# Paged attention on one core: copies of the cache spread differently over SyncE's and ScalarE's queues, and the first layer's weights of a row fetched whole

## The reference: what is computed

```python
# layer 0: each row picks one of 16 weights
x = x + einsum('bsi,boi->bso', x, weight[adapter_ids])          # 512 x 512 per row
# layer 1: attention with a paged cache
q, k, v = x @ Wq.T, x @ Wk.T, x @ Wv.T       # 32 query heads, 8 key heads, D = 128
q, k = rope(rmsnorm(q)), rope(rmsnorm(k))
kc, vc = k_cache[block_table], v_cache[block_table]   # 16 pages of 32 keys per row
scores = q @ concat(kc, k).T * SCALE         # 512 cached + 128 new keys, masked
x = x + (softmax(scores) @ concat(vc, v)) @ Wo.T
```

## Time and profile before

| | |
|---|---|
| median of 3 runs | 1103.47 us (1098.93 to 1104.15) |
| profiled execution | 1106.2 us |
| its span in the trace | 1104.4 us |
| TensorE busy | 1033.2 us, 94% of the span |
| VectorE, ScalarE, GpSimd busy | 79%, 73%, 69% |
| mean granted clock of TensorE | 0.978 |
| copies into `cache_rows` | 96 issued by SyncE, 32 by ScalarE |

### The profile page before, as it was taken

How to read it: one execution, slowest core, us unless ns; L and a number is a source line. 1 busy time by engine, 2 the same in 40 slices (tenths; PEclk the granted TensorE clock), 3 DMA queues, 4 the chain that set the end, 5 groups by cost and what they waited for, 6 DMA issues and landing times.

```text
span 1104.4 us, 19826 instructions
## 1 busy us (share of the span) xinstructions
PE 1033.2 (94%) x5500; PEld 877.1 (79%) x5500; DVE 868.8 (79%) x1999; ACT 803.2 (73%) x2094; POOL 758.8 (69%) x794
## 2 busy tenths in 40 slices
PE   7799897999999999999998999999998999899996
PEld 5587776888877888788887888788887888788874
DVE  6565555566887988898887998888898898888893
ACT  3364445555787887888787887888888887888883
POOL 1876656466476777877776776777777776777753
PEclk8999999899999999999999999999999999999999
DMA  6687767988667788788878887678877788777884
GB/s 202 185 251 233 213 185 202 242 246 212 132 139 151 141 162 149 137 152 147 159 138 148 145 162 151 144 145 147 161 144 151 143 159 148 138 147 141 149 154 98
DMA packets 477839, 180.87 MB, mean 164 GB/s; under 512 B 420753, under 2 KB 457762, under 8 KB 475682
## 3 DMA queue, kind: packets, MB, share of 16 engines
q1 hardware_dynamic: 474464, 167.61, 73.8%
q10 hardware_dynamic: 2242, 9.89, 2.9%
q0 software_dynamic: 1024, 2.10, 0.6%
HBM read 109.25 MB, written 35.66 MB: 131 GB/s over the span
## 4 chain that ended last, share of the span: by engine, by line
PE 52%; SPq 16%; DVE 11%; DMA 8%; issue 6%; POOL 4%; ACT 3%; POOLq 0%; DVEq 0%; ACTq 0%
PE S L1221 12%; PE O L1155 5%; SPq L394 5%; DVE pr L939 4%; SPq L349 4%; PE O L1156 4%; PE O L1157 4%; DMA first<-pr 4%; PE Q L1155 3%; PE Q L1157 3%; PE Q L1156 3%; POOL ptl L515 3%; SPq L404 3%; PE Y L1155 3%; PE Y L1157 3%
## 5 line engine op out<-in xcount | busy, mean ns | idle before, releaser
L921 DVE CUSTOM_DVE_ANT_0 pr<-S,mask,rst 128x640 f32<-128x640 f32 x256 | 225.5, 881 | 65.1 <-PE S L1221 58.9
L737 ACT ACTIVATE pr<-pr,nb 128x640 f32<-128x640 f32 x256 | 211.5, 826 | 32.0 <-DVE nb L921 31.6
L939 DVE SCALAR_TENSOR_TENSOR pr<-pr,rc,raw 128x640 f16<-128x640 f32 x208 | 229.7, 1105 | 5.0 <-ACT raw L722 4.9
L722 ACT ACTIVATE raw<-pr,rc 128x640 f16<-128x640 f32 x208 | 170.9, 822 | 0.1
L540 POOL TENSOR_TENSOR m<-m 128x512 f32<-128x512 f32 x64 | 111.4, 1740 | 70.4 <-DVE m L967 69.1
L1155 PE MATMUL O<-pth,vh 128*128 128x512 f32 x256 | 111.5, 436 | 40.5 <-POOL ptl L515 33.8
L494 POOL TENSOR_TENSOR kl<-raw,kh 128x512 fp32r<-128x512 f32 x64 | 97.6, 1526 | 66.5 <-ACT kh L622 65.2
L515 POOL TENSOR_SCALAR ptl<-first 128x512 fp32r<-128x512 f16 x130 | 94.0, 723 | 55.1 <-DMA first<-pr 46.6
L682 ACT ACTIVATE Q<-Q 128x128 f32<-128x128 f32 x256 | 68.2, 267 | 87.3 <-DVE m L967 87.3
L1221 PE MATMUL S<-kh,qh 128*128 128x320 f32 x512 | 122.3, 320 | 6.2 <-DVE nb L921 5.3
L515 POOL TENSOR_SCALAR ptl<-turned 128x512 fp32r<-128x512 f16 x130 | 96.5, 743 | 43.5 <-DMA turned<-pr 34.0
(11 more groups left out here) (114 smaller groups left out, 2778.9 us busy)
## 6 DMA issues: line engine op xcount, KB each, us to landing
raw<-cache_rows SPq DMA_DIRECT2D x112, 256.0 KB, 3.9
cache_rows<-in_kv SPq DMA_DIRECT2D x96, 256.0 KB, 4.9
wraw<-in_wall SPq DMA_DIRECT2D x73, 256.0 KB, 4.7
mask<-mask_rows SPq DMA_DIRECT2D x64, 128.0 KB, 3.5
cache_rows<-in_kv ACTq DMA_DIRECT2D x32, 256.0 KB, 5.6
first<-in_lw SPq DMA_DIRECT2D x28, 256.0 KB, 4.6
acc<-in_x SPq DMA_DIRECT2D x8, 256.0 KB, 4.7
raw<-in_kv SPq DMA_DIRECT2D x128, 16.0 KB, 3.1
```

The lines of the kernel that those rows point to most:

```text
L722: e.activation(upper16[:, g, :], pr[:, slot(u, g), :], ACT.Copy, scale=rc[:, u % 2, g:g + 1]).then_inc(a_f1, 1)
L737: e.activation(pr[:, slot(u, g), :], pr[:, slot(u, g), :], ACT.Exp, bias=nb[:, u % 2, g:g + 1], scale=-1.0, accum_out=sm[:, u % 2, g:g + 1 ...
L921: e.tensor_tensor_reduce(pr[:, slot(u, g), :].rearrange("p (a n) -> p a n", a=2), S[:, :, 0:320], mask[:, u % 2, :].rearrange("p (a n) -> ...
L939: e.scalar_tensor_tensor(out=lower16(u, g), in0=pr[:, slot(u, g), :], scalar=rc[:, u % 2, g:g + 1], in1=upper16[:, g, :], op0=ALU.mult, op ...
```

## The change

1. The table of copies: SyncE issues 20 groups and not 24, ScalarE 12 and not 8. Period by period, SyncE now issues fewer groups in periods 1, 3, 4 and 5; ScalarE issues two groups (eight transfers) in periods 1 to 5 and none in period 7.
2. ScalarE has eight registers for page numbers, loads two groups of numbers at its period's start, and issues up to two transfers in each of the four places.
3. The first layer's weights of rows 1 to 7 come in one transfer of 1 MB each with one semaphore; TensorE waits for it once, at the first of the row's four matmuls. Row 0 keeps its four transfers.

```diff
-COPY_SP = (1, 2, 1, 2, 1, 2, 2, 2, 3, 3, 3, 2)
-COPY_ACT = (1, 1, 1, 1, 1, 1, 1, 1, 0, 0, 0, 0)
+COPY_SP = (1, 1, 1, 1, 0, 1, 2, 2, 3, 3, 3, 2)
+COPY_ACT = (1, 2, 2, 2, 2, 2, 1, 0, 0, 0, 0, 0)
...
-        copy_regs = [nc.scalar.alloc_register(f"copied{j}") for j in range(4)]
+        copy_regs = [nc.scalar.alloc_register(f"copied{j}") for j in range(8)]
...
-                for t in range(4):
-                    e.dma_start(ws[:, t, :],
-                                lw[bass.ds(number, 1), t * P:(t + 1) * P, :].rearrange(
-                                    "a p n -> (a p) n")).then_inc(d_lw[b % 2][t], 16)
+                if b == 0:
+                    for t in range(4):
+                        e.dma_start(ws[:, t, :],
+                                    lw[bass.ds(number, 1), t * P:(t + 1) * P, :].rearrange(
+                                        "a p n -> (a p) n")).then_inc(d_lw[0][t], 16)
+                else:
+                    e.dma_start(ws, lw[bass.ds(number, 1)].rearrange(
+                        "a (t p) n -> p (a t) n", p=P)).then_inc(d_lw[b % 2][0], 16)
...
-                for b, t in copies_of(period, act=True):
+                for n, (b, t) in enumerate(copies_of(period, act=True)):
                     first_page = NPG * b + 4 * t
-                    e.load(copy_regs, page[0:1, first_page:first_page + 4])
-                    numbers = [e.snap(r, min_val=0, max_val=63) for r in copy_regs]
+                    regs = copy_regs[4 * n:4 * n + 4]
+                    e.load(regs, page[0:1, first_page:first_page + 4])
+                    numbers = [e.snap(r, min_val=0, max_val=63) for r in regs]
...
-                for place in copied[0:1]:
+                for place in copied[0:2]:
                     copy_page(*place)
...
-                e.wait_ge(d_lw[b % 2][t], 16 * (b // 2 + 1))
+                if b == 0 or t == 0:
+                    e.wait_ge(d_lw[b % 2][t], 16 * (b // 2 + 1))
```

More of the change, by code:

```diff
@@ L790, in _ @@
                     exp(i, 1)
-                for place in copied[1:2]:
+                for place in copied[2:4]:
                     copy_page(*place)
@@ L798, in _ @@
                     exp(i, 2)
-                for place in copied[2:3]:
+                for place in copied[4:6]:
                     copy_page(*place)
@@ L809, in _ @@
                     exp(i, 3)
-                for place in copied[3:4]:
+                for place in copied[6:8]:
                     copy_page(*place)
```

## The result

| | before | changed |
|---|---|---|
| first measurement, median | 1101.24 us (1098.93 to 1104.15) | 1088.87 us (1084.03 to 1090.6) |
| ratio, 95% interval | | 0.9879 (0.9835 to 0.9924) |
| second measurement, on another occasion, median | 1109.15 us (1103.99 to 1118.54) | 1092.29 us (1087.27 to 1092.84) |
| ratio, 95% interval | | 0.9823 (0.979 to 0.9857) |
| profiled execution, span | 1106.2 us, 1104.4 us | 1088.06 us, 1086.3 us |

Faster by 1.2% and by 1.8% in the two measurements. The forecast, 19.0 of 1103.5 us, is a ratio of 0.983: that of the second, and just outside the interval of the first. The first measurement alone could not have told the forecast from rival A: 12.4 us of gain is A's 12, and 1088.87 us lies in A's band of 1088 to 1096. What tells them apart is the trace. The two traces differ by 18.1 us of span.

A forecast was written before the change was run, and what follows sets the result against it. SyncE's issuing was taken to bound periods 3 to 6, TensorE the kernel as a whole. 20.8 us lost, minus 0.5 for ScalarE and 1.3 for periods 8 to 11, is 19.0: 1103.47 - 19.0 = 1084.5 us, range 1079.5 to 1094.

The forecast's parts named there:

- rival A: First twelve periods: transfers become the new wait above a 0.905 share; gain 12 us, 1088 to 1096 us; chance 16%.
- The bound and the ceiling: Between 87.6 and 204 us: SyncE's issuing bounds periods 3 to 6; at most 20.8 us can be won.
- The floor of 20.6 us: TensorE's undisturbed time for a period with first-layer product and transposition, 16.7 + 3.9 us.
- put at 17.1: Stretch from 158.6 us: TensorE's floor, 16.7 + 0.4, with the transposition in it but its first-layer product before it.
- The rounds: SyncE's rounds 3 to 6 begin near 96, 117, 133 and 153 us, round 7 at about 179.
- One issue of 1 MB: First-layer weights on SyncE: one issue taken as 0.5 us instead of four in 1.9 to 3.7; gain 8 us.
- The copies alone nearly suffice: If one 1 MB issue costs as much as four, page slacks of 5 to 10 us shrink by 1.6 to 4, still hold.
- ScalarE: Periods 1 to 5: four more issues, 2.4 us a period, mostly hidden; 0.1 a period taken, bounds nothing to 12 us.
- Rival C: Periods 1 to 5: ScalarE's queue fills at 1.91 us an issue; 11 us slower, 1114.5 us; chance 5%.
- Period 7, the term that was mis-sized: Stretch of period 7 falls to the 16.7 us floor; `load_k` of unit 8 landed at 167, wanted at 175.5.
- Periods 8 to 11: `load_k` of unit 9, landing in 7.7 to 13.1 us, stalls 0 to 1 us; another 0 to 2; 1.3 subtracted.
- Three microseconds of lead: Ahead of SyncE's round 1: weights of rows 1 to 3 gain some 5 us, 3 counted; start 56.5 instead of 59.4.

The follow-up runs named there:

- table of copies only: Kernel before with only the table of copies and ScalarE's eight registers changed, first-layer weights still in four transfers a row; 1094.41 us, 0.9852.
- grouped copies: Kernel before with SyncE's copies of rounds 0 to 5 issued as one 1 MB transfer a group, pages 0 to 15 in order; 1091.57 us, 0.9896.
- early split on the change: Changed kernel with VectorE splitting chunk 4 of head 1 at the end of period 6, not mid period 7; 1089.03, 1088.11 and 1085.60 us.
- idle loads: Changed kernel with the early split, plus twelve unused register loads a SyncE round, absent from the program that ran; 1088.78 us, 0.9856 to the kernel before.
- early split in the kernel before: Kernel before with only VectorE's split of chunk 4 of head 1 moved to the end of period 6; 1105.15 us, 1.001.
- more issues for SyncE: Changed kernel with the early split, plus eight unused 4-byte transfers in each of SyncE's rounds 1 to 5; 1095.31 us, 0.9929 to the kernel before.
- whole transfers only: Kernel before with only the first-layer weights in one transfer a row, table of copies as before; 1098.18 us, 0.9873.
- SyncE waits for the gather: Changed kernel with the early split; SyncE waits for GpSimd's unit 1 value gather before issuing row 3's weights; 1091.55 us, 0.9877 to the kernel before.
- gather earlier: Changed kernel with the early split; GpSimd issues both halves of unit 1's value gather together; 1084.96 us, 0.9833 to the kernel before.

## Why the prediction was right, point by point

*The bound and the ceiling.* That SyncE's issuing was late by its own length in periods 3 to 6 is shown from both sides: fewer issues with the same bytes bring 13.9 us, more issues with 32 bytes a round cost 9.7. The floor of 20.6 us was met in two stretches (20.60). The first stretch stayed at 21.20, and that of period 6, put at 17.1, is 17.57 in nearly every trace in which nothing waits.

*The rounds.* 96, 117, 133, 153 and 179 were forecast for rounds 3 to 7; they began at 95.8, 115.2, 132.6, 152.7 and 180.8.

*One issue of 1 MB.* Taken at 0.5 between 0.4 and 3.7; it is 0.38 to 0.41. "The copies alone nearly suffice" held: 14.7 us, with 5.3 us of waits for pages left. The other half alone left no waits for pages in its trace, but with TensorE late by 4.5 us itself; whether it frees them by itself stays open.

*ScalarE.* 0.5 us was taken for it, and 0 to 12 as bounds. All issues: 0.499 us in the median, 1.18 at most; no stretch of TensorE shows it. Rival C, which needed 1.6 us an issue, fell.

*The transfers.* Rival A took 0.905 as the highest share that TensorE could live with. Of the two stretches of 20.60 us one had 0.93, the other 0.80, and the one of 21.20 had 0.93. No wait for `raw<-in_kv`, `raw<-cache_rows` or a mask is left in either trace. The Trainium skill, "DMA: Bandwidth & Descriptors", section "Issuing engines are not separate DMA queues", says that issuing from more engines saves only the time to initiate; the runs agree: moving copies to ScalarE by itself brought 14.7 us, and saving issue time on SyncE without a second engine brought 13.9.

*Period 7, the term that was mis-sized.* The sum took 16.7 us for the stretch of period 7. It took 19.2 us in one trace of the changed kernel and 20.7 in the other, because VectorE splits a chunk there just ahead of TensorE's use. The wait for it stood in the trace of before, in the waits of all engines:

```profile
PE KV L1155 <- DVE wl L860: 4.4, 1, 4.4
```

The prediction left it out of the floor. This is 2.5 to 4.0 us of the sum; moving the split gave the 16.7.

*Periods 8 to 11.* 1.3 us were set aside, and none was needed: `load_k` of unit 9 landed in 6.9 us, below both values that were weighed.

*Period 1, which no step of the prediction had.* Three microseconds of lead were booked for SyncE ahead of round 1 as pure gain. The lead came (4.8 us), and with it the first-layer weights of row 3 moved from 51.8 to 49.5 us, ahead of the last quarter of GpSimd's gather of unit 1's values, which is issued at about 50. Over the traces, the time from the issue of that last quarter to the issue of the weights, and GpSimd's wait for the gather in period 1, are:

| kernel | weights after gather, us | GpSimd's wait, us |
|---|---|---|
| table of copies only | +2.2 | 0 |
| grouped copies | +2.1 | 1.4 |
| before | +1.2 | 0 |
| early split on the change: its three traces, and the same program with the idle loads | +0.7, +0.3, -0.4, -0.7 | 0.35, 1.5, 1.5, 3.2 |
| early split in the kernel before | 0.0 | 2.1 |
| more issues for SyncE | 0.0 | 1.9 |
| changed, two traces | -0.3, -0.4 | 2.9, 3.1 |
| whole transfers only | -0.3 | 4.7 |
| SyncE waits for the gather | +2.9 | 0 |
| gather earlier | +7.0 | 0 |

Where the weights come before the gather's last quarter, or less than 0.7 us after it, the gather is late, by 0.35 to 4.7 us. With more distance it is not, but for the 1.4 us of the grouped copies. The kernel before with the early split shows that four transfers do it as well as one, and that chance can bring the two together without the change. The change brings them together by making SyncE early. Both kernels that took them apart again, by a later transfer or by an earlier gather, lost the wait, in one trace each. TensorE's step there takes 5.5 us where nothing waits; it took 6.6 and 9.8 us in the two traces of the changed kernel, in the second of which the granted clock fell too (0.87 between 59.9 and 73 us), and 12.3 with whole transfers only. So the changed kernel's mark of period 2 lies at 87.9 in one trace and at 90.1 in the other. This doesn't explain why one change measured 1.2 and 1.8%: the 1.8% belong to the measurement whose trace has the later mark. What differs more there is the kernel before, 1101.24 and 1109.15 us.

Together, on the first trace: 20.8, less 2.5 for period 7, 0.6 for the first stretch (21.20 for 20.6), 0.5 for that of period 6 (17.57 for 17.1), 0.3 for the mark of period 2, which came later, and 0.2 for a mark that the ceiling took as 204.0 where it lies at 203.8, is 16.7. The 1.4 behind the mark of period 13 make it 18.1. So the forecast of 19.0 was 2.3 us above what these marks show (and 6 above the second trace's 13.0), by period 7 more than by all the rest. That it came no further off is partly luck: the ceiling was 4.1 too high, and the 1.8 set aside for ScalarE and for periods 8 to 11, of which nothing was needed, made up for part of it. The mechanism of SyncE's issuing was right.

## What to carry to other kernels

When the waits of a queue's own sequencer come to almost nothing over a long stretch while others wait for its transfers, its issue time is probably the bound, even beside a high DMA share (here 0.61 to 0.91). Here fewer issues and another sequencer each brought most of the gain. Then work out the floor of the engine behind it from undisturbed periods, but leave in the forecast every wait of the disturbed ones that the queue doesn't explain: here VectorE's split, 4.4 us before, was still a wait of 2.2 us after. And a queue that gets earlier starts its transfers earlier too, here beside a gather that had gone ahead of them.

## What the runs showed of the hardware

- The issue time of a transfer on SyncE's queue hardly depends on its size: in the traces of the changed kernel 0.38 to 0.41 us for 1 MB (512 pieces of 2 KB). Between places in DRAM it was 0.49 in the median for a copy of 256 KB (kernel before), 0.53 for one of 1 MB (grouped copies) and 0.54 for one of 4 bytes (more issues). All of these can take longer at times, up to 1.45 us for the 256 KB.
- On ScalarE the second of two issues in a row showed as 0.50 us of idle time before the next ACTIVATE, while the first lay under the one before it.
- Traces of one and the same program differ by a few microseconds in a stretch in which a gather and a large transfer meet: 6.6 and 9.8 us for one step of TensorE in the changed kernel (61.5 to 68.0, 60.4 to 70.2).
- 283 GB/s over a stretch of 20.6 us, at a DMA share of 0.93, left TensorE busy all of it.
